# A two-layer decoder for two sequences on one core: norms by column halves, stacks read by halves of the heads, and a new order of steps

## The chip, the core and the metric

The kernel runs on one core of a Trainium2 chip. The metric is the device time of one execution in microseconds, as the median of several runs. The profile shows one execution.

## The reference

The input is x, two sequences of 512 tokens with 128 features (f32), and a small context of 32 tokens per sequence. Two layers of three blocks each are applied, and each block stands inside a residual sum and a plain layernorm:

```python
x = _layernorm(x + L0_attn(x))     # rms norm, gated linear recurrence, rms norm, gated MLP
x = _layernorm(x + L0_xattn(x, ctx, mask))         # attention over the 32 context tokens
x = _layernorm(x + L0_ffn(x))      # x += latent attention(rmsnorm(x)), 16 heads, causal
                                   # x += experts(rmsnorm(x)): 1 shared, 7 routed, best 2
x = _layernorm(x + L1_attn(x))     # selective scan, 16 states
x = _layernorm(x + L1_xattn(x, ctx))  # norm, FiLM by context attention, long convolution
                                   # by FFT, then a norm with an MLP, then a norm
x = _layernorm(x + L1_ffn(x))      # experts: 2 shared, 8 routed, best 2
```

## The kernel before, in words

**Tiles.** A sequence is held feature-major, as tiles of 128 partitions (features) by 512 columns (tokens), f32. The two sequences are lanes a and b; work on weights that both share is lane w. Each lane a and b has four PSUM banks of 128x512, `own(b, 0)` to `own(b, 3)`, and SBUF tiles `A(b, i)`; `Xin[b]` is the running x (x_in in the profile).

**A norm.** A norm sums squares over the partitions. ScalarE (ACT) squares a tile (step `.sq`), TensorE (PE) multiplies it by a matrix of ones so that each partition holds the sum of its column (`.v` or `.ss`, L551-553), ACT takes Ln and then Exp with scale -0.5, which is the inverse root (`.l`, `.r`, L1077-1095), and VectorE (DVE) multiplies (L1418-1420). Two norms, m1 and f1, have an epsilon outside the root and take five steps on ACT (`.sq .l .n .m .r`, L1097-1107). The norms of a lane are h1, h4, ln1 (recurrent block), ln2 (context attention), m1, f1 and ln3 (latent attention and first experts), ln4 (scan), lni, lnf, lno, ln5 (state-space block) and ln6 (second experts). Each step works on the whole 128x512 tile. Ln, Exp, Gelu and Sin need tables that ACT loads by an instruction of its own (L1067).

**Stages of a lane.** Recurrent block (`hawk`); context attention (`xa.*`, a query product, exp, `xa.t`, the output product `xa.o`, the sum `s2`, ln2, `X2`); latents (m1, `lat`, `kf`, `q`); the split of keys and queries into bf16 parts, which SP writes to DRAM (`staged`, L489-496) and reads back as one stack of rows per side (`stacked`, L498-503); 40 max units per lane (`mx0.A` to `mx7.E`: eight pairs of heads, matmuls L688 and L691, DVE reductions L1407, L1549), from which a mask row is made (`nl`, `nmt`) and sent by a DMA; 40 score units `su` (L705, L708) with exp on ACT; first experts (f1, router `rt`, eight units of `fg`, `fu`, `fw`, `fd`, L775, L780, L791, L802, with an ACT step `sl` and DVE steps per unit); ln3; scan (sixteen states, `cn` L843, `bn` L849, `yn` L856 on PE, exp `aa` and copies `bb` on ACT, `by` on POOL (GpSimd), product and recurrence `sc`, L1719, `hc` on DVE); ln4; state-space block (`xb.s` L888, FiLM, Fourier products L870 and L923, centring products `lnf.c` and `ln5.c`, MLP `w1` and `w2`); second experts (14 units of `eg`, `eu`, `ew`, `ed`); ln6 and the store of x (L541-544).

**What sets the order.** Each engine runs one program in order. `STEPS` lists the steps of a lane on each engine; `TURNS` (L187-214) is a string per engine, "a6 w1 a6 ...", that says how the lanes take turns, and `take_turns` (L452-459) issues one step per turn. `TABLES` (L218-221) gives the numbers of the ACT steps ahead of which a table is loaded. Semaphores count the steps of each engine and lane; a step waits for counts. Lane b runs some way behind lane a throughout. SP issues its DMAs in the order of L460-544.

The stacks' reads and the store, as they stand:

```python
stacked("k", b, 0, 4, "hm", 2)
stacked("q", b, 0, 4, "hm", 3)
stacked("k", b, 4, 6, "l", 1)
stacked("q", b, 4, 6, "l", 1)
...
for b in range(B):
    sp.wait_ge(*after("dve", b, "X6"))
    sp.dma_start(out[:, b * T:(b + 1) * T], Xin[b][:, :]).then_inc(stored, 16)
```

## Time and profile before

| | us |
|---|---|
| runs (device time) | 523.45, 525.23, 526.22; median 525.23 |
| the profiled execution | 523.02 |
| its span in the trace | 521.2 |
| PE busy | 442.6 (85% of the span) |
| DVE busy | 362.8 (70%) |
| ACT busy | 288.2 (55%) |
| POOL busy | 127.7 (24%) |
| mean granted TensorE clock | 0.948 of full |

Times in the rows are counted from the span's start. A row of the timeline reads: start, duration, engine, line, operation, output and input tiles with shapes, count, and in brackets the idle time of the engine ahead of it and what released it; consecutive instructions of one kind are one row. A row of the view of groups reads: line, engine, operation, tiles, count, then busy time in us, the mean of one in ns, and the idle time ahead of them with its releasers. A row of the view by stretches of time reads: stretch, its length, busy time (and count of instructions) of PE, PEld (weight loads), DVE, ACT and POOL, then the granted TensorE clock, the share of the DMA engines in use and GB/s. Stretches follow the stages: up to 112.0 the recurrent blocks and context attention of both lanes; to 147.2 a's max units; to 153.0 the mask row of a; 193.5 to 238.7 a's attention done, b's score units with a's first experts; 277.8 the end of a's `dl`, when a's scan begins; 309.6 a's `sc7`; 373.6 b's scan ends; 383.0 b's query product `xb.s`; 423.0 the state-space blocks are done; 514.0 the last expert product.

### The profile page before, as it was taken

The page shows a single profiled execution, that of the slowest core. Times are in us where ns is not written, and L with a number is a line of the kernel's source. Part 1 is how long each engine was busy: PE and PEld are TensorE (multiplying, and loading weights), DVE is VectorE, ACT ScalarE, POOL GpSimd, SP SyncE. Part 2 cuts the span into 40 slices and gives each one's busy share as a digit, 9 for nine tenths or more (in the row PEclk, how much of TensorE's full clock was granted, in tenths as well). Part 3 has the DMA queues.
Part 4 walks back from the last instruction along what each step waited for, and adds up shares of the span by engine and source line. Part 5 has one row for each costly group of instructions (what it writes and reads, how often), then busy time and mean ns, then how long its engine had stood idle before and what let it go on. Part 6 is the DMA issues. An engine that isn't in the chain of part 4 may idle for free.

```text
span 521.2 us, 5808 instructions
## 1 busy us (share of the span) xinstructions
PE 442.6 (85%) x2045; PEld 203.5 (39%) x2045; DVE 362.8 (70%) x625; ACT 288.2 (55%) x443; POOL 127.7 (24%) x128
## 2 busy tenths in 40 slices
PE   6979879478849989999778797778979889999996
PEld 3534423233325534343333332333645434444441
DVE  1496875548937946645988898999694462695774
ACT  5637884431125557887557968686347344722124
POOL 2100000001940009318406868656200000000000
PEclk9999999678769999999999989999989989999998
DMA  8940001830820000004000000160000000000001
GB/s 289 305 148 6 1 1 60 181 133 7 221 24 1 1 6 2 0 2 126 37 1 0 1 1 0 20 241 1 1 0 1 0 0 1 1 0 0 1 1 40
DMA packets 10279, 24.29 MB, mean 47 GB/s; under 512 B 3103, under 2 KB 7936, under 8 KB 9088
## 3 DMA queue, kind: packets, MB, share of 16 engines
q1 hardware_dynamic: 10148, 23.82, 15.4%
q8 instruction: 16, 0.26, 0.2%
q14 instruction: 13, 0.11, 0.1%
q10 hardware_dynamic: 102, 0.10, 0.1%
HBM read 19.88 MB, written 3.67 MB: 45 GB/s over the span
## 4 chain that ended last, share of the span: by engine, by line
PE 54%; DVE 23%; ACT 15%; issue 5%; DMA 2%; DVEq 0%; ACTq 0%
ACT AR L1071 10%; DVE AR L1398 6%; PE PS L802 6%; PE PS L780 6%; PE PS L775 6%; DVE stats L1407 4%; DVE AR L1404 4%; PE PS L705 3%; PE PS L719 3%; ACT L1067 3%; PE PS L589 3%; PE PS L553 3%; DVE AR L1719 3%; PE PS L688 2%; PE PS L870 2%
## 5 line engine op out<-in xcount | busy, mean ns | idle before, releaser
L1071 ACT ACTIVATE AR<-PS 128x512 f32<-128x512 f32 (+1 forms) x201 | 113.1, 593 | 108.9 <-PE PS L775 47.3
L2026 POOL TENSOR_TENSOR AR<-AR 128x512 f32<-128x512 f32 (+2 forms) x48 | 54.2, 1139 | 90.7 <-DVE AR L1398 68.6
L1071 ACT ACTIVATE AR<-AR 128x512 f32<-128x512 f32 (+2 forms) x72 | 43.9, 618 | 51.9 <-DVE AR L1398 34.1
L1398 DVE TENSOR_TENSOR AR<-PS,AR 128x512 f32<-128x512 f32 x74 | 50.4, 687 | 13.8 <-ACT AR L1071 6.4
L1407 DVE TENSOR_REDUCE stats<-PS 128x1 f32<-128x512 f32 (+4 forms) x88 | 43.2, 525 | 13.4 <-PE PS L691 8.1
L1404 DVE SCALAR_TENSOR_TENSOR AR<-AR,PS 128x512 f32<-128x512 f32 x44 | 30.0, 683 | 21.7 <-ACT AR L1071 21.6
L1067 ACT ACT_TABLE_LOAD x33 | 42.3, 1283 | 0.6
L2119 POOL TENSOR_TENSOR RR<-KL,lags 128x512 f32<-128x512 f32 x24 | 31.0, 1324 | 46.5 <-PE PS L708 46.4
L1719 DVE TENSOR_TENSOR_SCAN AR<-PS,AR 128x512 f32<-128x512 f32 x32 | 38.9, 1217 | 2.9 <-ACT PS L1071 2.7
L705 PE MATMUL PS<-RR 100*128 100x512 bf16 (+3 forms) x128 | 31.9, 323 | 7.9 <-DMA RR<-wT 5.5
L688 PE MATMUL PS<-RR 97*128 97x512 bf16 (+3 forms) x128 | 33.4, 335 | 4.0 <-DVE stats L1407 3.1
L856 PE MATMUL PS<-AR,W_sq 128*128 128x512 f32 x64 | 33.8, 610 | 1.8 <-DVE AR L1398 1.8
L1404 DVE SCALAR_TENSOR_TENSOR AR<-PS,AR 128x512 f32<-128x512 f32 x44 | 29.9, 687 | 7.5 <-PE PS L791 4.8
L553 PE MATMUL PS<-AR,W_sq 128*128 128x512 f32 x44 | 25.6, 666 | 10.5 <-ACT AR L1071 10.3
L775 PE MATMUL PS<-x_in,RR 128*128 128x512 f32 x56 | 28.9, 607 | 1.1 <-DVE AR L1404 1.1
L1071 ACT ACTIVATE AR<-PS,W_vec 128x512 f32<-128x512 f32 (+1 forms) x32 | 22.2, 696 | 12.7 <-PE PS L553 7.3
L802 PE MATMUL PS<-AR,RR 128*128 128x512 f32 x56 | 28.5, 593 | 0.2 <-DVE AR L1404 0.2
L780 PE MATMUL PS<-x_in,RR 128*128 128x512 f32 x56 | 27.9, 594 | 0.0
L1398 DVE TENSOR_TENSOR AR<-AR 128x512 f32<-128x512 f32 (+4 forms) x36 | 24.4, 694 | 3.8 <-ACT AR L1071 3.3
L1071 ACT ACTIVATE PS<-AR,W_vec 128x512 f32<-128x512 f32 x32 | 22.0, 690 | 6.5 <-DVE AR L1719 6.4
L691 PE MATMUL PS<-W_bf 128*128 128x256 bf16 (+1 forms) x80 | 22.0, 275 | 0.0
L1549 DVE TENSOR_REDUCE stats<-PS 128x1 f32<-128x384 f32 x32 | 17.6, 550 | 5.2 <-PE PS L691 5.2
(239 smaller groups left out, 768.7 us busy)
## 6 DMA issues: line engine op xcount, KB each, us to landing
RR<-in_ffn SPq DMA_DIRECT2D x1, 2688.0 KB, 9.2
RR<-in_ones SPq DMA_DIRECT2D x2, 832.0 KB
RR<-in_ones SPq DMA_DIRECT2D x2, 784.0 KB
RA<-in_moe SPq DMA_DIRECT2D x1, 1539.5 KB, 6.3
W_mla<-in_mla SPq DMA_DIRECT2D x1, 1504.0 KB, 16.4
W_late<-in_late SPq DMA_DIRECT2D x1, 1076.0 KB, 10.5
RA<-in_xa SPq DMA_DIRECT2D x1, 1056.0 KB, 8.7
RA<-in_hawk SPq DMA_DIRECT2D x1, 1024.0 KB, 10.8
```

The lines of the kernel that those rows point to most:

```text
L688: mm(ring[:, c:c + n_], Qst[b][0:MROWS, h, 128 * qt:128 * qt + 128], Kst[b][0:MROWS, h, 0:n_], start=(qt, c) == segs[0][1:], stop=False)
L705: mm(ring[:, c:c + n_], Kst[b][0:KROWS, h, 128 * kb:128 * kb + 128], Qst[b][0:KROWS, h, 128 * kb:T], start=(c == 0), stop=False)
L775: mm(own(b, 0), w(group, "g", 128 * k, 128), x, start=True, stop=True)\
L780: mm(own(b, 1), w(group, "u", 128 * k, 128), x, start=True, stop=True)\
L802: mm(own(b, 3), w(group, "d", 128 * j, 128), A(b, 6 + j % 2), start=(j == 0 and base is None), stop=(k == n))\
L1067: nc.scalar.preload_act_table_set(tables[loaded[0]])
L1071: nc.scalar.activation(out_, in_, func, bias=bias, scale=scale).then_inc(*done("act", *step))
L1398: nc.vector.tensor_tensor(out_, a, b_, op).then_inc(*done("dve", *step))
L1404: nc.vector.scalar_tensor_tensor(out_, a, s1, b_, op0, op1).then_inc(*done("dve", *step))
L1407: nc.vector.tensor_reduce(out_, a, X, op).then_inc(*done("dve", *step))
L1719: nc.vector.tensor_tensor_scan(A(b, 14 + i % 2), own(b, 3), A(b, 4 + i % 3), 0.0, ALU.mult, ALU.add).then_inc(*done("dve", b, f"sc{i}"))
L2026: nc.gpsimd.tensor_tensor(out_, a, b_, op).then_inc(*done("pool", *step))
```

## The change

- `COLS` names two halves of the columns: "a" for 0 to 255, "" for 256 to 511. Every norm but lni works on them step by step: squares, the product with ones, Ln, Exp, and the DVE multiply are two instructions of 128x256 each. The two halves' sums go into two different PSUM banks of the lane (`NORM_BANKS`). The five-step norms m1 and f1 take ten ACT steps.
- The DVE sums ahead of norms (`s2`, `s4`, `xt`, `s5`, `s6`), the centred products `lnf.x` and `lno.x`, the centring matmuls `lnf.c` and `ln5.c`, and the affine `lnf.g` are halved too. The norms whose input is one product of PE (`shr`, `fd7`, `w2`) wait for the whole of it.
- The last x is stored by four DMAs of 128 KB, one per lane and half, instead of two of 256 KB.
- The stacks are read by halves of the heads: first heads 0 to 7 of all four row groups, then heads 8 to 15, with a semaphore of their own (`second`), for which PE waits ahead of pair 4 of the max units. That is eight DMAs per lane instead of four, with the same bytes.
- `TURNS` and `TABLES` are new. Steps per engine (lanes a and b and w together): PE 611 to 637, DVE 584 to 618, ACT 409 to 491, POOL 96 as before. Table loads by `TABLES`: 33 to 34.

The places where the new order differs most:

- PE: `a.mx0.A` and `a.mx0.B` come before `b.xa.t0` (they were behind `b.xa.o`); `b.mx0.A` to `C` come before `a.su0`; b's mask row is made after `a.su26` (was `a.su32`). By `b.su39` only `a.rt`, `fg0`, `fu0` of a's experts have been issued (before: `fg`, `fu` up to 3, `fw`, `fd` up to 2). The scan of a starts when b has about 8 DVE steps of its experts left (19 before); b's scan starts after `a.sc7` (before: after `a.sc15`). b's `w1`, `w2` come ahead of a's second experts. Lane b is alone from `eg9` (before: from `eg5`), since a's `ln6` and store come before b's last units.
- ACT: the log table is loaded ahead of `a.ln1.l`, another ahead of `b.h4.l`, sin ahead of `b.h4.sq` (early part); all ten steps of b's f1 with two table loads and the shared `sQ0` stand between `a.sl1` and `a.sl2`; log is loaded ahead of `a.ln6.l` and exp again ahead of `b.el10`.
- DVE: the shared centring `v0.s`, `v0.m`, `v0.c` and `k1`, `bi`, `vr` stand in part ahead of `a.gh1` and `a.x1`; b's convolution taps stand behind `a.X1` and `a.xa.m0`.
- POOL: b's split comes before `bf`, `bf1`, `se`, `wz`, `la` and `dc1` of lane w.

```diff
+COLS = (("a", slice(0, HT)), ("", slice(HT, T)))
+NORM_BANKS = {"h1": (0, 1), "h4": (1, 2), "ln1": (1, 2), "ln2": (1, 2), "f1": (0, 3), "ln3": (1, 0), "ln4": (1, 3),
+              "lnf": (3, 0), "lno": (3, 1), "ln5": (3, 2), "ln6": (1, 0), "lnf.c": (2, 1), "ln5.c": (0, 1)}
...
-            def mean_square(b, t, i, step="v"):
-                pe.wait_ge(*after("act", b, f"{t}.sq"))
-                mm(own(b, i), w("sq", "ones"), A(b, 1), start=True, stop=True).then_inc(*done("pe", b, f"{t}.{step}"))
+            def mean_square(b, t, step="v"):
+                for i, (h, c) in zip(NORM_BANKS[t], COLS):
+                    pe.wait_ge(*after("act", b, f"{t}.sq{h}"))
+                    mm(own(b, i)[:, c], w("sq", "ones"), A(b, 1)[:, c], start=True, stop=True)\
+                        .then_inc(*done("pe", b, f"{t}.{step}{h}"))
+                    yield
...
+            def layernorm(b, t, engine, ready, src, bias=0, whole=False):
+                for h, c in COLS:
+                    act.wait_ge(*after(engine, b, ready if whole else ready + h))
+                    f(A(b, 1)[:, c], src(h)[:, c], ACT.Square, (b, f"{t}.sq{h}"), bias=bias)
+                    yield
+                for i, (h, c) in zip(NORM_BANKS[t], COLS):
+                    act.wait_ge(*after("pe", b, f"{t}.v{h}"))
+                    f(A(b, 7)[:, c], own(b, i)[:, c], ACT.Ln, (b, f"{t}.l{h}"), scale=1.0 / D, bias=vec("eps"))
+                    yield
+                for h, c in COLS:
+                    act.wait_ge(*after("act", b, f"{t}.l{h}"))
+                    f(A(b, 7)[:, c], A(b, 7)[:, c], ACT.Exp, (b, f"{t}.r{h}"), scale=-0.5)
+                    yield
...
             def normed(b, t, name, src):
-                dve.wait_ge(*after("act", b, f"{t}.r"))
-                tt(Xin[b][:, :], src, A(b, 7), ALU.mult, (b, name))
+                for h, c in COLS:
+                    dve.wait_ge(*after("act", b, f"{t}.r{h}"))
+                    tt(Xin[b][:, c], src[:, c], A(b, 7)[:, c], ALU.mult, (b, name + h))
+                    yield
...
-                stacked("k", b, 0, 4, "hm", 2)
-                stacked("q", b, 0, 4, "hm", 3)
-                stacked("k", b, 4, 6, "l", 1)
-                stacked("q", b, 4, 6, "l", 1)
+                sp.wait_ge(draft["k", b, "hm"], 16 * 2)
+                stacked("k", b, 0, 4, 0)
+                sp.wait_ge(draft["q", b, "hm"], 16 * 3)
+                stacked("q", b, 0, 4, 0)
+                sp.wait_ge(draft["k", b, "l"], 16)
+                stacked("k", b, 4, 6, 0)
+                sp.wait_ge(draft["q", b, "l"], 16)
+                stacked("q", b, 4, 6, 0)
+                for which in "kq":
+                    stacked(which, b, 0, 4, 1)
+                    stacked(which, b, 4, 6, 1)
...
                 for pair in PAIRS:
+                    if pair == len(PAIRS) // 2:
+                        pe.wait_ge(second["k", b], 16 * 2)
+                        pe.wait_ge(second["q", b], 16 * 2)
...
-                sp.wait_ge(*after("dve", b, "X6"))
-                sp.dma_start(out[:, b * T:(b + 1) * T], Xin[b][:, :]).then_inc(stored, 16)
+                for h, c in COLS:
+                    sp.wait_ge(*after("dve", b, f"X6{h}"))
+                    sp.dma_start(out[:, b * T + c.start:b * T + c.stop], Xin[b][:, c]).then_inc(stored, 16)
...
-        "a6 w1 a6 w2 a1 w1 a8 w1 a1 w2 a2 b1 a3 b2 a1 b2 a2 b4 a2 b1 a2 b8 a1 b1 a3 b1 a1 b10 a2 b1 a10 b1 a3 "
+        "a7 w1 a6 w1 a1 w1 a1 w1 a7 w1 a2 w2 a2 b1 a1 b1 a2 b1 a1 b1 a1 b2 a2 b3 a2 b1 a2 b2 a1 b7 a1 b2 a4 b9 "
...
```

## Rows read from the trace of the kernel before

**Rows 1.** Busy time by stretches of the span, one row per stage.

```profile
94.90:112.00 17.10, 11.38 (x29) 6.04 (x29) 7.26 (x13) 2.90 (x6) 0.00 (x0) 0.50 0.54 92
112.00:147.20 35.20, 27.46 (x124) 10.51 (x122) 31.56 (x69) 8.39 (x13) 16.84 (x28) 0.84 0.54 141
147.20:153.00 5.80, 1.24 (x7) 0.71 (x8) 0.00 (x0) 1.19 (x2) 2.16 (x2) 0.50 0.03 8
...
193.50:238.70 45.20, 43.03 (x299) 19.46 (x300) 25.34 (x45) 38.02 (x63) 23.14 (x18) 0.96 0.00 1
238.70:277.80 39.10, 30.64 (x230) 12.87 (x229) 31.80 (x56) 23.45 (x33) 13.30 (x11) 1.00 0.17 55
277.80:309.60 31.80, 28.86 (x74) 11.67 (x73) 27.62 (x36) 23.69 (x33) 27.27 (x23) 0.95 0.00 1
309.60:373.60 64.00, 51.54 (x313) 24.37 (x312) 59.60 (x71) 43.79 (x72) 38.98 (x29) 1.00 0.15 54
373.60:383.00 9.40, 5.88 (x33) 4.34 (x34) 6.84 (x9) 3.93 (x6) 0.00 (x0) 0.93 0.00 0
383.00:423.00 40.00, 35.58 (x124) 20.50 (x124) 23.05 (x40) 19.95 (x29) 0.00 (x0) 0.93 0.00 0
423.00:514.00 91.00, 89.20 (x228) 38.53 (x227) 60.53 (x112) 34.22 (x51) 0.00 (x0) 1.00 0.00 1
514.00:521.20 7.20, 2.25 (x4) 0.59 (x4) 2.08 (x3) 3.21 (x6) 0.00 (x0) 0.79 0.19 73
```

**Rows 2.** Timeline of the norm h4 of lane a, from squares to multiply.

```profile
37.09 0.63 ACT L1071 ACTIVATE AR<-AR 128x512 f32<-128x512 f32 x1 [6.52 <-DVE AR L1398]
...
38.09 1.12 PE L553 MATMUL PS<-AR,W_sq 128*128 128x512 f32 x2
...
39.25 0.60 ACT L1071 ACTIVATE AR<-PS 128x512 f32<-128x512 f32 x1 [1.53 <-PE PS L553]
...
39.88 0.63 ACT L1071 ACTIVATE AR<-AR 128x512 f32<-128x512 f32 x1
...
40.54 0.75 DVE L1404 SCALAR_TENSOR_TENSOR AR<-AR,W_vec 128x512 f32<-128x512 f32 x1 [1.50 <-ACT AR L1071]
```

**Rows 3.** Groups of instructions, by shape: prices at 512 and at 256 columns.

```profile
L1071 ACT ACTIVATE AR<-PS 128x512 f32<-128x512 f32 x197 | 111.4, 595 | 105.6 <-PE PS L775 47.3 <-PE PS L708 21.5 <-PE PS L849 10.8
...
L1071 ACT ACTIVATE AR<-PS 128x256 f32<-128x256 f32 x2 | 0.6, 371 | 0.0
...
L1398 DVE TENSOR_TENSOR AR<-PS,AR 128x512 f32<-128x512 f32 x74 | 50.4, 687 | 13.8 <-ACT AR L1071 6.4 <-PE PS L606 2.5 <-PE PS L780 2.1
...
L1398 DVE TENSOR_TENSOR stats<-stats 128x256 f32<-128x256 f32 x6 | 2.4, 421 | 0.1
...
L553 PE MATMUL PS<-AR,W_sq 128*128 128x512 f32 x44 | 25.6, 666 | 10.5 <-ACT AR L1071 10.3
...
L923 PE MATMUL PS<-RR,AR 128*128 128x256 f32 x32 | 8.9, 431 | 0.0
...
L1067 ACT ACT_TABLE_LOAD x33 | 42.3, 1283 | 0.6
```

**Rows 4.** Timeline: last stack read of lane a, `b.xa.t0`, first max unit of a.

```profile
95.46 0.42 SPq L503 DMA_DIRECT2D RR<-draft_q  x1
...
104.05 1.11 PE L636 MATMUL PS<-W_sq,AR 128*128 128x128 f32 x4 [3.11 <-DVE AR L1398]
...
110.18 0.15 PEld L688 LDWEIGHTS PS<-RR 97*128 97x128 bf16 x1 [0.52 <-issue]
```

**Rows 5.** Timeline: PE's first score unit of lane a, behind the mask row.

```profile
152.39 0.61 PE L705 MATMUL PS<-RR 100*128 100x512 bf16 x1 [4.56 <-DMA RR<-wT]
```

**Rows 6.** Timeline: a table load between steps of b's f1; POOL's shared work in the scan.

```profile
252.27 1.28 ACT L1067 ACT_TABLE_LOAD   x1
...
285.31 4.06 POOL L2119 TENSOR_TENSOR RR<-KL,lags 128x512 f32<-128x512 f32 x4
```

**Rows 7.** Timeline: PE's product `xb.s` of lane b, behind its norm ln4.

```profile
380.89 0.49 PE L888 MATMUL PS<-M,x_in 128*128 128x128 f32 x2 [3.52 <-DVE x_in L1398]
```

More of the change, by code:

```diff
@@ L141 @@
[L141 removed]
+        *_halves("ln4.v"), "xb.s", "xb.t", "fl0", "fl1", "fl2", "fl3", "xit",
+        "xf0", "xf1", "inv0", "inv", *_halves("lnf.c"), *_halves("lnf.v"), "w10", "w11", "w12", "w13", "w2", *_halves("lno.v"), *_halves("ln5.c"), *_halves("ln5.v"),
         "rt1", *[x for k in range(UB1 + 1) for x in unit_steps(k, UB1, SH1, "e")],
[L143 removed]
+        *_halves("ln6.v")],
     "act": [
[L145 removed]
@@ L299, in build @@
                   "sel1", "km", "kr", "tm"]}
+        second = {(w, b): ctx.enter_context(nc.semaphore(f"second_{w}{b}")) for w in "kq" for b in range(B)}
         stack = {(w, b): ctx.enter_context(nc.semaphore(f"stack_{w}{b}")) for w in "kqm" for b in range(B)}
@@ L858, in scan @@
                         yield
[L859 to L860 removed]
+                yield from mean_square(b, "ln4")
             def forward(o, p, x):
@@ L926, in state_space @@
                     yield
-                pe.wait_ge(*after("dve", b, "xt"))
-                mm(own(b, 2), w("sq", "Cm"), A(b, 0), start=True, stop=True).then_inc(*done("pe", b, "lnf.c"))
-                yield
-                mean_square(b, "lnf", 3)
-                yield
+                for i, (h, c) in zip(NORM_BANKS["lnf.c"], COLS):
+                    pe.wait_ge(*after("dve", b, f"xt{h}"))
+                    mm(own(b, i)[:, c], w("sq", "Cm"), A(b, 0)[:, c], start=True, stop=True)\
+                        .then_inc(*done("pe", b, f"lnf.c{h}"))
+                    yield
+                yield from mean_square(b, "lnf")
                 pe.wait_ge(*after("act", b, "lnf.g"))
@@ L946, in state_space @@
                 yield
-                mean_square(b, "lno", 3)
-                yield
-                pe.wait_ge(*after("dve", b, "lno.x"))
-                mm(own(b, 1), CmG, A(b, 9), start=True, stop=True).then_inc(*done("pe", b, "ln5.c"))
-                yield
-                mean_square(b, "ln5", 0)
-                yield
+                yield from mean_square(b, "lno")
+                for i, (h, c) in zip(NORM_BANKS["ln5.c"], COLS):
+                    pe.wait_ge(*after("dve", b, f"lno.x{h}"))
+                    mm(own(b, i)[:, c], CmG, A(b, 9)[:, c], start=True, stop=True).then_inc(*done("pe", b, f"ln5.c{h}"))
+                    yield
+                yield from mean_square(b, "ln5")
             def second_experts(b):
@@ new lines, in root_mean_square @@
+            def root_mean_square(b, t):
+                for i, (h, c) in zip(NORM_BANKS[t], COLS):
+                    act.wait_ge(*after("pe", b, f"{t}.ss{h}"))
+                    f(A(b, 7)[:, c], own(b, i)[:, c], ACT.Ln, (b, f"{t}.l{h}"), scale=1.0 / D)
+                    yield
+                for h, c in COLS:
+                    act.wait_ge(*after("act", b, f"{t}.l{h}"))
+                    f(A(b, 7)[:, c], A(b, 7)[:, c], ACT.Exp, (b, f"{t}.r{h}"), scale=-0.5)
+                    yield
@@ L1152, in hawk @@
                     yield
-                yield from layernorm(b, "ln1", "pe", "shr", own(b, 0), 1)
+                yield from layernorm(b, "ln1", "pe", "shr", lambda h: own(b, 0), whole=True)
             def context_attention(b):
@@ L1247, in first_experts @@
                 yield from gates(b, U0, SH0, "f", "sl", "h", "wt", E0)
-                yield from layernorm(b, "ln3", "pe", f"fd{U0}", own(b, 3), 1)
+                yield from layernorm(b, "ln3", "pe", f"fd{U0}", lambda h: own(b, 3), whole=True)
             def scan(b):
@@ L1318, in state_space @@
                 yield
-                yield from layernorm(b, "lnf", "pe", "lnf.c", own(b, 2), 3)
-                affine(b, "lnf", 9, 2, "gff", "bff")
-                yield
+                yield from layernorm(b, "lnf", "pe", "lnf.c", lambda h: own(b, NORM_BANKS["lnf.c"][0 if h else 1]))
+                for h, c in COLS:
+                    affine(b, "lnf", 9, 2, "gff", "bff", h, c)
+                    yield
                 for k in range(4):
@@ L1325, in state_space @@
                     yield
-                yield from layernorm(b, "lno", "pe", "w2", own(b, 2), 3, b2c)
-                yield from layernorm(b, "ln5", "dve", "s5", A(b, 0), 0)
+                yield from layernorm(b, "lno", "pe", "w2", lambda h: own(b, 2), b2c, whole=True)
+                yield from layernorm(b, "ln5", "dve", "s5", lambda h: A(b, 0))
             def second_experts(b):
```

260 lines of the change are left out of this document (126 added, 134 removed), and 52 rows, old and new, of tables (STEPS, TABLES, TURNS).

## The prediction

> **What bounds the kernel.** I first split the span into stages and read, in the view by stretches, which engine fills each one [rows 1]. No engine bounds the whole. In a's attention with b's score units PE is full (43.03 of 45.2 us), and in the second experts again (89.20 of 91). DVE is full in a's max units (31.56 of 35.2) and in the scans (27.62 of 31.8, 59.60 of 64.0), and it is the busiest engine of the first experts' stretch (31.80 of 39.1). Nobody is full in three places: 94.9 to 112.0, where PE works 11.38 of 17.1 us at half clock (1.2 GHz); 147.2 to 153.0, the wait for a's mask row; and around the norms of b at 373.6 to 383.0 and of both lanes up to 423.0. There the chain of one norm sets the time. So I read a norm in the timeline [rows 2]: squares at 37.09, the multiply done at 41.29, 4.2 us for five instructions on three engines, each waiting for the one before it. A shorter chain pays only where no engine is full. That is the whole question.
>
> **What a half costs.** ACT takes 595 ns for 512 columns and 371 for 256, DVE 687 and 421, a matmul pass of PE 666 and 431 [rows 3]. Two halves thus cost 147 ns more than the whole on ACT and 155 on DVE. A chain in halves: squares 2 x 0.37, then PE's second half, 0.43 and the hand-over (the wait of 1.53 us for a product of two passes, of which 1.12 are busy, so 0.41 + 2 x 0.3, as the passes overlap: about 1.0), then Ln, Exp, multiply of the second half, 0.37 + 0.39 + 0.45. That is 2.95, with a little queueing 3.1: **1.1 us gained per exposed chain** of the 4.2. Between 0 (an engine in the chain is busy with other steps, or the input comes whole) and 1.9 (the next product starts on its first half, which no reader of the whole tile does). I take 1.1, nearest to the row.
>
> The Trainium skill, "VectorE: DVE Perf Modes", section on the TRN2 errata, speaks against the change: operations that read SBUF on VectorE and ScalarE pay a fixed cost per instruction, and tiles of 512 elements or more are advised. The durations of 371 and 421 ns agree with a fixed part. By that advice alone the change would be a loss of the extra busy time, which the next paragraph prices from rows.
>
> The extra busy time is 82 x 0.147 = 12.1 us on ACT and 34 x 0.155 = 5.3 on DVE. ACT is full nowhere [rows 1], so its part costs only inside chains, where the 3.1 has it. Of DVE's, some 12 of the 34 pairs lie in stretches where DVE is full: about 1.9 us, in the terms below.
>
> **Part by part, along the span.**
>
> 1. *Start to 112.0.* Four chains of a and four of b are crossed, in part hidden by the other lane; I count 4 x 1.1 = 4.4 gained. Against it: two table loads move into chains (2 x 1.28 [rows 3] = 2.6), the shared centring stands on DVE ahead of `a.x1` (about one step of 0.7), and b's taps behind `a.X1` hold `a.xa.m0`'s successors for about 1.0. Net 0, between -3 (the loads fall into waits) and +2. `a.mx0.A` and `B` now stand ahead of `b.xa.t0` on PE. Before, `b.xa.t0` ran at 104.05, and the last read of a's stacks was issued at 95.46 [rows 4], while the first max unit came at 110.18. If the stacks come later than b's exps, everything of b behind them waits; half-stacks are half the bytes, so I take this as nothing, up to +2 inside this term.
> 2. *112.0 to 147.2.* DVE-bound. b's latents no longer stand in its way as whole tiles, and two waits of DVE on chains (3.6 idle of 35.2) shrink: -1.5, between -2.5 and 0.
> 3. *147.2 to 153.0.* a's mask row. PE idles 4.56 us for it [rows 5]. `b.mx0.A` to `C` now stand in that hole, because half of b's stacks suffices. a's 40 max units fill 35.2 us with 27.46 of PE [rows 1], so three are 2.1 us of PE, taken out of a later stretch where PE is full; half of it, as the mask row also has to be made with b's units in its way: -1.0, between -4.6 and 0.
> 4. *Experts and scans, 193.5 to 373.6.* Two units of a's experts and the first two products of a third move from ahead of `b.su39` to behind it. In the second experts 28 units fill 89.2 us of PE, 3.2 each [rows 1], so that is at most 2 x 3.2 + 2 = 8.4; 7.5 taken, since those 89.2 hold a router and norms too. The attention becomes shorter by them and the stretch behind longer. In that one PE has 39.1 - 30.64 = 8.5 idle, so in principle they fit; but b's f1 takes ten half steps (10 x 0.38), two loads (2 x 1.28 [rows 6]) and `sQ0` (1.9) on ACT between `a.sl1` and `a.sl2`: 8.3 us in which a's experts get no sigmoid part. The five steps of f1 in halves gain nothing in length, as each engine step waits for ACT anyway. In the scan, POOL's shared pieces stand as a block of 4.06 [rows 6] between a's `by`. DVE, which is the bound, has the same work, and the two experts side by side give it more to choose from, which gives back some. Net +1.5, between -3 and +7.5 (nothing of the moved work fits).
> 5. *ln4 of b, to 383.0.* PE waited 3.52 for it [rows 7], and in the stretch DVE and PE are both part idle. Sum, squares, product, root and multiply in halves: 1.1, and 0.5 more as `s4` is halved too, and b comes out of the scan with less left of a's work in the way. -2, between -3.5 and 0.
> 6. *383.0 to 423.0.* PE is idle 4.4 of 40.0 [rows 1], on lnf, lno and ln5. Three chains of each lane with centring and affine in halves, of which two are exposed: -2, between -4.4 and 0.
> 7. *End.* a's ln6 products move into the PE-bound stretch (the whole one is 1.12 busy [rows 2]: +0.9), two table loads (2.6) stand between `b.el9` and `b.el10` where a unit lasts 3.2, which covers most (+0.7), and the tail of 7.2 us [rows 1] holds one lane's norm in halves and stores of 128 KB (-1.3). +0.3, between -1.3 and +1.6.
>
> The reads by halves alone (term 1 and 3) I cost at nothing: the last was issued 14.7 us ahead of the first use [rows 4], and the bytes are the same.
>
> **Sum.** 0 - 1.5 - 1.0 + 1.5 - 2 - 2 + 0.3 = -4.7. The profiled execution took 523.0, so 518.3 in its terms. It lies 2.2 below the median of the runs, 525.2. I forecast **520.5 us**, 0.9% below the median. What this measurement can tell from no change is 0.5%, that is 522.6 to 527.9.
>
> **Rivals.**
> - *The clock comes back (chance 0.17).* From 94.9 to 112.0 the clock is half, with PE busy 11.38 us [rows 1]. If the max units drawn forward keep PE at work, and the full 2.4 GHz stays, up to 5.7 us of this falls away, and the hole at 147.2 may go as well. For it: max units are the one work that is ready. Against it: the chains of b still stop PE, and two units are short. Term 1 at -4 and term 3 at -3.2 give 6.2 less: 514.3.
> - *Halves give back what they gain (0.20).* The exposed chains are hidden by the other lane already, DVE pays its 5.3, and terms 2, 3, 5 and 6 (6.5) come out at half while term 4 costs 3: 525.2 - 3.2 + 3 + 0.3 = 525.3, no difference. It holds too if the change does not do what it says: reads by halves of stacks that had long been issued.
> - *a's experts are late (0.23).* Slower. One mechanism: term 4 at its bound. The 8.3 us of ACT between `a.sl1` and `a.sl2` lie on a's path, `a.dl` comes up to 7.5 later, and the scans, where DVE is full for 87.2 of 95.8 us, can't take it back. It decides from the point at which `a.dl` comes later than 281. Then term 4 is +7.5, the others at half of their gain (-3.1): 525.2 + 4.4 = 529.6.
>
> **How the numbers follow.** Forecast 0.40, clock 0.17, no difference 0.20, late experts 0.23. Faster by over 0.5% is the forecast and the clock, 0.57; within it 0.20; slower 0.23. The range: the clock's case and term 5 and 6 at their better ends (2.4 and 1.5 less) reach 510.4, and the late experts with term 1 at +2 reach 531.6. So 510 to 532, with less than 2 in 10 outside. The forecast's own range is 516 to 524.
>
> **What would show it.** In the changed kernel: ACT groups of 128x256 near 0.37 to 0.40 us and a norm of about 3.1 us from first square to last multiply (term by chain); `b.s2` within 2 us of 112; PE's idle time ahead of the first score unit below 4; `a.dl` at 276 to 281; DVE still over 90% busy in the scans; the wait ahead of `xb.s` below 2.5; the tail from the last product at about 6. The forecast falls if `a.dl` is past 281 and the scans don't make up for it, if the stretch around 95 to 112 shows full clock, or if PE waits for DMA ahead of `b.xa.t0`.

## The result: 1.2% slower, and the profile after

The changed kernel's median is 530.95 us (527.53 to 536.00, 9 runs), the kernel before's 524.96 (520.94 to 526.53, 9 runs beside it). The ratio is 1.0121, with a 95% interval of 1.0089 to 1.0152. The forecast was 520.5, 0.9% faster. The time lies inside the range of 510 to 532, on the wrong side of no change, and within 1.5 us of the rival "a's experts are late" (529.6, chance 0.23).

Two of the changed kernel's nine runs, 535.49 and 536.00, are over 1.5% above its fastest, count as slow and are left out of the ratio; the other seven lie within 5.5 us (527.53 to 533.02), as far apart as the 5.6 of the kernel before. The profiled execution took 530.81 us, with a span of 529.0. The two profiles differ by 7.8 us and the medians by 6.0, since the profile before was a quick one; the times by steps below are those of the profiles.

The view by stretches for the changed kernel follows, with stretches that end at the same steps as those of [rows 1] where the same step ends one: `b.s2` at 118.8, a's mask row from DVE at 152.8, `a.su0` at 158.6, `a.su39` at 203.5, `b.su39` at 230.5, `a.dl` at 288.4, the end of a's scan (348.1) and of b's (384.5), `b.xb.s` at 392.3, then up to 432, to the last product (523.0) and to the end. The columns are those of [rows 1].

```profile
101.70:118.80 17.10, 10.73 (x30) 5.12 (x29) 7.49 (x15) 4.57 (x10) 0.00 (x0) 0.61 0.58 106
118.80:152.80 34.00, 26.53 (x124) 11.40 (x125) 31.75 (x70) 8.53 (x21) 16.62 (x30) 0.85 0.56 146
152.80:158.60 5.80, 2.98 (x14) 1.57 (x15) 1.64 (x4) 1.19 (x2) 4.98 (x8) 0.50 0.03 8
158.60:203.50 44.90, 42.27 (x376) 22.54 (x377) 26.04 (x63) 28.88 (x53) 0.00 (x0) 0.98 0.01 2
203.50:230.50 27.00, 25.42 (x217) 11.84 (x210) 10.93 (x20) 21.84 (x47) 12.15 (x12) 1.00 0.01 2
230.50:288.40 57.90, 51.21 (x288) 22.46 (x288) 52.06 (x93) 34.39 (x53) 20.53 (x18) 1.00 0.12 37
288.40:348.10 59.70, 43.90 (x199) 16.95 (x200) 53.70 (x60) 40.74 (x63) 50.34 (x39) 0.86 0.00 1
348.10:384.50 36.40, 32.35 (x202) 18.95 (x188) 32.49 (x43) 22.93 (x41) 14.58 (x10) 1.00 0.27 94
384.50:392.30 7.80, 5.10 (x20) 3.57 (x20) 6.17 (x10) 4.25 (x9) 0.00 (x0) 0.77 0.00 0
392.30:432.00 39.70, 35.26 (x139) 22.91 (x139) 21.49 (x39) 23.58 (x45) 0.00 (x0) 0.96 0.00 1
432.00:523.00 91.00, 89.22 (x236) 39.81 (x234) 62.56 (x127) 38.11 (x63) 0.00 (x0) 1.00 0.01 3
523.00:529.00 6.00, 1.13 (x4) 0.67 (x4) 1.50 (x4) 2.26 (x6) 0.00 (x0) 0.98 0.13 44
```

The kernel before has these rows for the two attentions and the scans, cut at the same steps (its stretch from `b.su39` to `a.dl` stands in [rows 1]):

```profile
153.10:195.80 42.70, 40.06 (x331) 21.38 (x330) 28.33 (x66) 24.77 (x44) 0.00 (x0) 0.94 0.01 2
195.80:238.70 42.90, 40.76 (x289) 18.05 (x288) 25.34 (x45) 36.83 (x61) 23.14 (x18) 0.98 0.00 1
...
277.80:333.40 55.60, 45.59 (x243) 18.16 (x241) 49.44 (x61) 41.41 (x60) 45.09 (x37) 0.97 0.01 2
333.40:373.60 40.20, 34.81 (x143) 17.88 (x143) 37.79 (x46) 26.07 (x45) 21.17 (x15) 1.00 0.23 82
```

Every step counts a semaphore, so the trace tells when each step ended. The difference of these times says where the 7.8 us of span went:

| step | before | after | difference | gained or lost since the step above |
|---|---|---|---|---|
| `a.g3` (gate products of a) | 23.73 | 28.34 | +4.61 | +4.6 |
| `b.s2` | 112.04 | 118.80 | +6.76 | +2.2 |
| `a.nl` (mask row of a, DVE) | 147.16 | 152.72 | +5.56 | -1.2 |
| `a.su0` | 153.11 | 158.64 | +5.53 | 0.0 |
| `a.dl` | 277.80 | 288.37 | +10.57 | +5.0 |
| `b.hc15` (b's scan on DVE) | 373.56 | 384.45 | +10.89 | +0.3 |
| `b.xb.s` | 383.06 | 392.28 | +9.22 | -1.7 |
| `b.X6` | 518.76 | 526.72 | +7.96 | -1.3 |

Two stretches lose: the start (+6.8), and the way from `a.su0` to the end of the scans (+5.4). The rest gains 4.2. These are differences from one profile before to one after. How far a difference can be trusted is seen in the other traces of the study, wherever their order is the same in the stretch; where they change the reading, it is said below.

The halves themselves cost what the forecast's rows said. From the groups by shape:

```profile
L1093 ACT ACTIVATE AR<-PS 128x256 f32<-128x256 f32 x26 | 9.3, 378 | 4.8 <-PE PS L952 2.4 <-PE PS L828 1.1 <-PE PS L639 0.7
...
L578 PE MATMUL PS<-AR,W_sq 128*128 128x256 f32 x88 | 27.9, 429 | 13.0 <-ACT AR L1093 8.6 <-DMA W_sq<-in_sq 4.4
...
L1431 DVE TENSOR_TENSOR x_in<-AR 128x256 f32<-128x256 f32 x16 | 6.3, 420 | 5.2 <-ACT AR L1093 5.2
```

And the norm h4 of lane a, in the timeline, is the chain of [rows 2]:

```profile
42.20 0.72 ACT L1093 ACTIVATE AR<-AR 128x256 f32<-128x256 f32 x2 [7.02 <-DVE AR L1431]
...
42.67 1.13 PE L578 MATMUL PS<-AR,W_sq 128*128 128x256 f32 x4 [0.60 <-ACT AR L1093]
...
43.41 0.82 ACT L1093 ACTIVATE AR<-PS 128x256 f32<-128x256 f32 x2 [0.48 <-PE PS L578]
...
44.12 0.71 ACT L1093 ACTIVATE AR<-AR 128x256 f32<-128x256 f32 x2
44.56 0.88 DVE L1437 SCALAR_TENSOR_TENSOR AR<-AR,W_vec 128x256 f32<-128x256 f32 x2 [1.21 <-ACT AR L1093]
```

It takes from 42.20 to 45.44, 3.24 us instead of 4.20. PE's idle time ahead of the product with ones is 0.60, and ACT's ahead of Ln is 0.48 instead of 1.53.

### The profile page after: what moved, and what is told of

It reads as the page before. It is cut to its first block, busy times and chain, and to the rows that moved or that the text cites. A ratio compares the mean times of both kernels' runs of the same rounds, so it can differ in the third digit from the quotient of the medians.

```text
span 529.0 us, 6043 instructions
## 1 busy us (share of the span) xinstructions
PE 448.7 (85%) x2097; PEld 216.3 (41%) x2097; DVE 367.2 (69%) x659; ACT 296.2 (56%) x526; POOL 122.1 (23%) x128
## 4 chain that ended last, share of the span: by engine, by line
PE 53%; DVE 23%; ACT 13%; issue 6%; DMA 2%; SPq 1%; ACTq 0%; DVEq 0%
ACT AR L1093 9%; DVE AR L1431 6%; PE PS L801 5%; PE PS L828 5%; PE PS L806 4%; DVE stats L1440 4%; DVE AR L1437 4%; PE PS L880 3%; PE PS L615 3%; PE PS L728 3%; ACT L1089 3%; PE PS L742 3%; PE PS L893 2%; PE PS L578 2%; DMA x_in<-in_x 2%
## 5 line engine op out<-in xcount | busy, mean ns | idle before, releaser
L1093 ACT ACTIVATE AR<-PS 128x512 f32<-128x512 f32 (+1 forms) x213 | 114.5, 575 | 127.5 <-PE PS L801 60.4
L1093 ACT ACTIVATE AR<-AR 128x256 f32<-128x256 f32 (+3 forms) x114 | 48.4, 462 | 46.5 <-DVE AR L1431 30.6
L1431 DVE TENSOR_TENSOR AR<-PS,AR 128x512 f32<-128x512 f32 (+1 forms) x76 | 50.1, 670 | 14.0 <-ACT AR L1093 5.4
L2160 POOL TENSOR_TENSOR RR<-KL,lags 128x512 f32<-128x512 f32 x24 | 25.5, 1100 | 67.2 <-PE PS L731 45.3
L578 PE MATMUL PS<-AR,W_sq 128*128 128x256 f32 x88 | 27.9, 429 | 13.0 <-ACT AR L1093 8.6
L880 PE MATMUL PS<-AR,W_sq 128*128 128x512 f32 x64 | 35.1, 639 | 0.0
L728 PE MATMUL PS<-RR 100*128 100x512 bf16 (+3 forms) x128 | 29.6, 305 | 3.1 <-ACT AR L1093 2.3
L1431 DVE TENSOR_TENSOR AR<-AR 128x512 f32<-128x512 f32 (+4 forms) x36 | 25.5, 723 | 6.6 <-ACT AR L1093 6.0
L1093 ACT ACTIVATE AR<-PS,W_vec 128x256 f32<-128x256 f32 (+2 forms) x48 | 25.0, 549 | 8.4 <-PE PS L578 4.1
L578 PEld LDWEIGHTS PS<-AR,W_sq 128*128 128x128 f32 x88 | 16.0, 203 | 28.4 <-ACT AR L1093 21.0
```

What stands on the lines that cost most here:

```text
L578: mm(own(b, i)[:, c], w("sq", "ones"), A(b, 1)[:, c], start=True, stop=True)\
L728: mm(ring[:, c:c + n_], Kst[b][0:KROWS, h, 128 * kb:128 * kb + 128], Qst[b][0:KROWS, h, 128 * kb:T], start=(c == 0), stop=False)
L880: mm(own(b, 2), w("sq", "Cm"), A(b, 12 + (i - 1) % 2), start=(i == 1), stop=(i == NS))\
L1093: nc.scalar.activation(out_, in_, func, bias=bias, scale=scale).then_inc(*done("act", *step))
L1431: nc.vector.tensor_tensor(out_, a, b_, op).then_inc(*done("dve", *step))
```

## Where the start lost 4.6 us

In the timeline of the changed kernel, DVE, ACT and PE stand like this between 13 and 28 us. The second block is PE's row in the kernel before:

```profile
13.65 0.43 DVE L1446 CAST AR<-kmask 128x512 f32<-128x512 uint8 x1 [5.23 <-DMA tmask<-in_tm]
14.04 0.42 ACT L1093 ACTIVATE AR<-x_in 128x256 f32<-128x256 f32 x1 [6.30 <-DMA x_in<-in_x]
19.52 8.80 PE L615 MATMUL PS<-AR,RA 128*128 128x512 f32 x16 [3.72 <-DVE AR L1437]
```

```profile
16.61 7.11 PE L589 MATMUL PS<-AR,RA 128*128 128x512 f32 x16 [0.86 <-DVE AR L1404]
```

Two steps of other lanes stand ahead of a's convolution in the new order, and each waits for a DMA: on DVE the cast of a mask, `w.km`, ahead of a's taps, and on ACT the first half of b's square, `b.h1.sqa`, ahead of the two copies `a.cv0`, `a.cv1` that the taps read. The engines run in order, so lane a waits with them. Its gate products start 2.9 us late, and the same 16 matmul passes then take 8.80 us instead of 7.11. The granted clock says why. The two blocks are the view by stretches from 19 to 24 us, after and then before; the granted clock is 0.66 of full in the one and 1.00 in the other:

```profile
19.00:24.00 5.00, 4.48 (x7) 1.97 (x8) 0.83 (x2) 2.83 (x7) 0.00 (x0) 0.66 0.93 224
```

```profile
19.00:24.00 5.00, 5.00 (x14) 2.09 (x14) 0.69 (x1) 3.94 (x8) 1.42 (x4) 1.00 0.94 207
```

## Experiments

Each kernel is built from one of the two by a change of the order or of the code. "Halves" is the code of the changed kernel. Where an order of one kernel is used with the code of the other, a whole step stands where its second half stood, or two halves side by side where the whole stood. Each ratio is to the kernel before as it ran beside that experiment, with a median from 521.03 to 524.98 us; it is estimated from the single runs, so it isn't the exact quotient of two medians.

**Halves alone.** The changed code in the old order.

```diff
 # code of the changed kernel
-TURNS, TABLES of the changed kernel
+TURNS, TABLES of the kernel before, each halved step's turn doubled
```

> All halves, the two banks, the stacks read by halves and the four stores, in the order of before (each pair of half steps stands where the whole step stood, table loads as before). Theory 'order' (the new order of steps costs the time): the halves gain what exposed chains gave in the forecast, about 1.1 us per exposed norm, so about 520, 1% below before. Rival 'halves' (their fixed costs, 12 us of ACT and 5 of DVE, make the loss): about 530, as the changed kernel.

Measured: 521.50 us, ratio 0.9988 (0.9965 to 1.0011). The halves are not the loss. Over the whole kernel they are no gain that can be told either, though 1% was expected.

**Order alone.** The code of before in the new order.

```diff
 # code of the kernel before
-TURNS, TABLES of the kernel before
+TURNS, TABLES of the changed kernel, the turn of each first half taken out
```

> The new order and table loads with whole norms, whole stacks and two stores (each whole step stands where its second half stood). Theory 'order': slower than the changed kernel, since nothing is gained on the chains: 533 or more. Rival 'halves': as before, 525.

Measured: 536.62 us, ratio 1.0294 (1.0257 to 1.0331). The loss is the order's. In the new order the halves are worth 1.0294 - 1.0121 = 1.7%, in the old one 0.1%. One thing differs from the changed kernel besides the halves: b's first square stands here behind a's copies, where its second half stood, and a's gate products end at 24.80, not at 28.34. So this 2.9% holds little of the wait at the start.

That can be read in the length of the chains, from the end of the step that feeds a norm to the end of its multiply, in us:

| chain | before | order alone | both (changed) | halves alone |
|---|---|---|---|---|
| a: `x1` to `xn2` (h4) | 4.23 | 3.92 | 3.27 | 3.80 |
| a: `shr` to `X1` (ln1) | 4.77 | 6.27 | 6.24 | 4.84 |
| b: `xa.o` to `X2` (ln2) | 4.90 | 6.08 | 6.88 | 4.49 |
| a: `x2a` to `xf` (f1) | 7.72 | 11.77 | 12.11 | 7.65 |
| b: `yn16` to `X4` (ln4) | 6.10 | 4.75 | 3.77 | 6.17 |
| b: `xt` to `lnf.g` (lnf) | 10.76 | 7.63 | 4.66 | 8.32 |
| b: `ed14` to `X6` (ln6) | 4.75 | 4.74 | 3.77 | 4.47 |

Side by side in the old order a chain gains 0.4 us at h4 and ln2, 0.3 at ln6, 2.4 at lnf, and nothing at ln1 and ln4, where other work of ACT or DVE stands in it. At ln4 and ln6 only the new order gives the halves their 1 us (4.75 to 3.77, 4.74 to 3.77). The same new order makes other chains longer: ln1 of a, because a table load of 1.28 us (at 55.62) and a shared Tanh (`th`, 0.30) stand in it, and f1 of a, by 4.4 us, because the score units of b come first.

The lengths of whole stretches add what the chains don't show. From the end of b's scan to `b.X6`, the kernel before takes 145.2 us, halves alone 143.0, order alone 148.0 and the changed kernel 142.3. Behind the scans the halves are thus worth 2.2 us in the old order too, and the new order adds 0.7 with them and costs 2.8 without. The clock has a part in it: in all five traces of kernels without halves PE stands at half clock for 3.4 or 6.8 us from a point between 418 and 430 us, where the state-space blocks hand over to the second experts, and in none of the eleven with halves. Halves alone give their 2.2 us back ahead of that: `a.su0` is 1.0 later than before, and the way from there to the end of the scans 1.2 longer (221.6 against 220.4), both within what traces of one order differ by.

**The mask cast put back, in the changed kernel.** TURNS of DVE.

```diff
-a2 w1 a6 w1 a2 w8 ...
+a8 w2 a2 w8 ...
```

> The changed kernel with one shared DVE step, the cast of a mask (km), put back behind lane a's six convolution taps. The trace of the changed kernel shows DVE waiting 5.23 us for the mask's DMA in front of it, and the gate products of a ending 4.6 us later. Theory 'order', first part: the 4.6 us are carried to the end nearly whole, so 4 us less, about 527. Rival 'covered later': the delay is taken up by the waits behind it (DMA of the stacks, mask row), so under 1 us less, 530 to 531.

Measured: 530.92 us, ratio 1.0161 (1.0124 to 1.0198). No gain. In its trace the taps start where ACT's copies let them, and the gate products are still 4.3 us late. PE waits 3.19 us ahead of them.

**The mask cast moved forward, in the kernel before.** TURNS of DVE.

```diff
-a7 w2 a2 w8 ...
+a1 w1 a6 w1 a2 w8 ...
```

> The kernel before with that one step moved ahead of lane a's convolution taps, nothing else. Theory 'order', first part: 4 us more, about 529. Rival 'covered later': within 1 us of before.

Measured: 526.59 us, ratio 1.0095 (1.0064 to 1.0126). The medians show the expected loss. In its trace only 1.1 us of it stand at `a.g3` and at `a.su0` (24.82 and 154.24); where the rest arises isn't shown.

**Both put back, in the changed kernel.** TURNS of DVE as above, and of ACT.

```diff
-a1 w1 a3 w1 a2 b1 w1 a2 ...
+a1 w1 a3 w1 a2 w1 a2 b1 ...
```

> The changed kernel with two early steps put back: the mask cast behind a's taps on DVE, as in the run before, and b's first half square (h1.sqa) behind a's two convolution copies on ACT, where the kernel before had it. In the trace of the changed kernel ACT waits 6.3 us for b's x in front of those copies, and everything of lane a stands behind it. Theory 'early wait': a's gate products end 4 us sooner, and 3 to 4 us of it reach the end, so about 527.5 against 531. Rival 'covered later': a's start is early but a.su0 comes no sooner than 157, and the end moves by less than 1.5 us.

Measured: 528.14 us, ratio 1.0057 (1.0023 to 1.0091), about 3.4 us better than the changed kernel (1.0121; the intervals just meet). PE now waits 0.86 ahead of the gate products:

```profile
16.24 3.67 PE L614 MATMUL PS<-AR,RA 128*128 128x512 f32 x8 [0.86 <-DVE AR L1436]
```

But these are the first 8 passes only, and `a.g3` still ends at 25.00, 1.3 us later than in the kernel before. A third step of another lane is in the way:

```profile
17.68 0.31 ACT L1092 ACTIVATE AR<-AR 128x128 f32<-128x128 f32 x1 [3.14 <-DMA AR<-in_s4d]
18.00 1.28 ACT L1088 ACT_TABLE_LOAD   x1
...
21.29 3.70 PE L614 MATMUL PS<-AR,RA 128*128 128x512 f32 x8 [1.38 <-ACT AR L1092]
```

It is `w.dt`, an Exp on state-space weights that a DMA still brings. In the new order it stands, with a table load, ahead of a's two Gelu steps `gg0` and `gg1`, and the third gate product waits for `gg1`. In the kernel before, `w.dt` comes behind them and ends at 21.00, and `gg1` at 16.39, not 21.25. No run puts this step back alone.

**The square alone put back, in the changed kernel.** The ACT line of the edit above.

> The changed kernel with b's first half square (h1.sqa) behind a's two convolution copies on ACT; the mask cast stays early. Theory 'ACT waits for b's x': all of the gain of the run with both moved, ratio to before about 1.006 against 1.012 to 1.016, so 3 us less than the changed kernel. Rival 'both needed': DVE waits for the mask in its place, and under 1 us is won.

Measured: 531.60 us, ratio 1.0116 (1.0077 to 1.0155). No gain that can be told, though its interval meets that of the run with both put back. The traces say it more sharply: the first gate product (`a.g0`) ends at 22.68 in the changed kernel, at 21.66 with the cast put back, at 21.67 with the square put back, and at 18.21 with both (18.58 before). So the rival holds, "both needed": either wait by itself holds the taps, and taking one away uncovers the other.

**The square moved forward, in the kernel before.** TURNS of ACT.

```diff
-a1 w1 a3 b1 a3 w3 ...
+a1 w1 a1 b1 a5 w3 ...
```

> The kernel before with b's square h1.sq ahead of a's two convolution copies on ACT, nothing else. Theory 'ACT waits for b's x': the copies wait for the DMA until 14 us instead of starting near 12, PE idles in front of the gate products and drops to the lower clock; 3 to 5 us slower, ratio 1.006 to 1.010. Rival 'covered later': under 1 us.

Measured: 529.83 us, ratio 1.0093 (1.0056 to 1.0130). One ACT step two places earlier costs as much in the medians as the mask cast did. The gate products of these two runs, of the square's and then of the cast's:

```profile
20.51 6.18 PE L587 MATMUL PS<-AR,RA 128*128 128x512 f32 x7 [4.80 <-DVE AR L1402]
```

```profile
17.70 7.10 PE L587 MATMUL PS<-AR,RA 128*128 128x512 f32 x16 [2.36 <-DVE AR L1402]
```

With 2.36 us of idle time PE kept its clock (7.10 us for the 16 passes, as before); with 3.33 (square alone put back, 8.74 us for 16), 3.72 and 4.80 it came back at a lower one.

**Old order up to a's first score unit, then the new one.** Halves.

```diff
+order[e] = old[e][steps done at 153.5 us] + new[e][the rest]
```

> Halves throughout; up to the first score unit of a (153 us) each engine's order of before, and from there the order of the changed kernel (steps already done left out). Theory 'both parts lose': the early 5.5 us are gone, the later part loses as in the changed kernel, so 525 to 527. Rival 'early part alone': 521.5, as halves in the old order. Rival 'late part alone': 530.

Measured: 525.76 us, ratio 1.0025 (1.0006 to 1.0044).

**New order up to there, then the old one.** Halves.

```diff
+order[e] = new[e][steps done at 158.0 us] + old[e][the rest]
```

> The mirror of it: halves; up to a's first score unit the order of the changed kernel, from there the order of before. Theory 'both parts lose': 526 to 528 (5.5 us from the early part, less what b's max units, which are ahead, give back). Rival 'early part alone': 530. Rival 'late part alone': 521.5.

Measured: 527.75 us, ratio 1.0081 (1.0045 to 1.0116). Against halves alone (0.9988) the early part costs 0.9% and the late one 0.4%, and together they make 1.3%, as in the changed kernel. The late 0.4% is small for its noise, as the intervals of this pair just meet (1.0006 and 1.0011). The length from `a.su0` to the end of the scans is clearer: 221.6, 221.7 and 223.3 us in three traces with halves and the old order there, 225.8 to 227.9 in six with the new one. So both parts lose.

**Old order up to the end of b's attention, then the new one.** Halves.

```diff
+order[e] = old[e][steps done at 239.6 us] + new[e][the rest]
```

> Halves; the order of before up to b's last score unit (239.6 us), the order of the changed kernel from there. Theory 'DVE work moved out of the attention' (in the changed order the DVE does 37 us of work during both attentions against 54 before, and the 17 us come back in a stretch where DVE is full): with the old order up to here nothing is moved, so no later than halves alone, 521 to 522, or a little less as the new order's tail is shorter. Rival 'order of experts and scans' (the two experts side by side, b's f1 chain on ACT, POOL's pieces): 525 or more, as when the new order starts at 153.

Measured: 537.97 us, ratio 1.0284 (1.0248 to 1.0320). The expected 521 to 522 are missed; the rival's "525 or more" is met, but by 13 us more. The trace shows that this hybrid makes a mismatch of its own. In the old attention a's experts have come to `sl3` when b's last score unit ends (236.40 and 237.51). The new order is written for a b whose score units end 18.6 us ahead of `a.sl3`. It puts b's f1 norm, its two table loads and `b.sl0` ahead of `a.sl4` on ACT:

```profile
246.60 0.72 ACT L1090 ACTIVATE AR<-AR 128x256 f32<-128x256 f32 x2 [2.73 <-DVE AR L1428]
247.34 1.28 ACT L1086 ACT_TABLE_LOAD   x1
...
252.27 1.28 ACT L1086 ACT_TABLE_LOAD   x1
...
260.16 0.60 ACT L1090 ACTIVATE AR<-PS 128x512 f32<-128x512 f32 x1 [2.54 <-PE PS L798]
```

`a.sl4` ends at 260.8, 16.5 us later than in the kernel before, and `a.dl` at 294.6. It says that the order of the experts only fits the attention that it was written with; it does not say what that order costs in its own place.

**New attention alone.** Halves; old up to `a.su0`, new up to `b.su39`, then old.

```diff
+order[e] = old[e][to 153.5 us] + new[e][to 226.7 us] + old[e][the rest]
```

> Halves; old order up to a's first score unit, the changed kernel's order up to b's last score unit (226.7 us), then the old order. Theory 'DVE work moved out of the attention': 524 to 526, all of the late loss. Rival 'order of experts and scans': 521.5.

Measured: 525.71 us, ratio 1.0053 (1.0025 to 1.0082). By the medians the new order of the attentions alone costs as much as the whole late part did (1.0025, the intervals meet). By the traces it is about half: from `a.su0` to the end of the scans 224.0 us, against 221.6 in halves alone and 226.8 with the whole late part new. So the order of the experts and scans has a share too, and no run measures that in its own place. The stretches of this run, from `a.su39` on, cut at `b.su39`, at `a.dl` and at the end of the two scans:

```profile
198.10:225.20 27.10, 25.52 (x218) 11.91 (x218) 10.89 (x21) 22.22 (x48) 12.15 (x12) 1.00 0.01 2
225.20:280.30 55.10, 43.36 (x260) 18.56 (x259) 43.02 (x83) 34.56 (x51) 19.56 (x16) 0.94 0.13 39
280.30:335.80 55.50, 45.58 (x246) 18.63 (x244) 49.62 (x62) 41.64 (x63) 45.13 (x37) 0.97 0.01 3
335.80:377.00 41.20, 34.86 (x144) 18.33 (x144) 38.83 (x48) 26.24 (x48) 20.89 (x15) 1.00 0.22 80
```

b's attention is over 13.5 us sooner than before, counted from `a.su0`, with the same small share of DVE as in the changed kernel (10.89 of 27.1). Behind it DVE has 131.5 us of work in 151.8, against 119.0 in 134.9. That is 87% of the stretch and not more than the 88% before: the stretch grows by 16.9 us with 12.5 us more of DVE work, so DVE's work explains most of its growth but not all.

**b.v ahead of the mask row, in the changed kernel.** TURNS of ACT.

```diff
-... b5 a5 b31 a1 b1 a29 b1 a3 ...
+... b5 a5 b32 a30 b1 a3 ...
```

> The changed kernel with one ACT step moved: the copy of b's values (b.v), whose product is there at 134.8, ahead of a's mask row copy (a.nmt) instead of behind it and its DMA issue. In the trace of the changed kernel b's first max unit waits for it until 156.2, so that only three units fit into the hole. Theory 'b.v holds the units back': they start 2.7 us sooner and their DVE steps too, DVE idle of 4.25 falls to under 2; worth 0.5 to 1 us at the end if DVE's part counts, 0 if not, since PE's next step waits for the mask row anyway. Rival: slower by the copy of 0.6 us ahead of the mask row, no, since ACT waits 13 us there; so none.

Measured: 532.12 us, ratio 1.0140 (1.0094 to 1.0185), no different from the changed kernel. b's first max unit does end earlier (4.6 us ahead of the end of `a.su0` instead of 1.7), and no gain follows from it.

**Halves in the old order, with five max units in the hole.** TURNS of PE and ACT.

```diff
-pe:  ... a3 b4 a28 b1 a2 b1 a1 b1 a2 b1 a1 b2 a2 b2 ...
+pe:  ... a3 b4 a26 b5 a8 b1 a2 b2 ...
-act: ... b2 a1 b27 a1 b1 a37 b1 a4 ...
+act: ... b2 a1 b28 a38 b1 a4 ...
```

> Halves in the order of before, with b.v ahead of a.nmt on ACT and five of b's max units (mx0.A to E) ahead of a's first score unit on PE, where before stood none; nothing else. The first halves of b's stacks landed at 144.5 in the run of halves alone, so five units of about 0.6 us fit into the 4.6 us in which PE waits for the mask row. Theory: 5 x 0.55 = 2.7 us of PE leave the attention, where PE is full, so 518.5 to 519.5, 0.5% under before. Rival 'DVE or the mask row sets it': no difference to halves alone, 521.5.

Measured: 521.59 us, ratio 0.9967 (0.9948 to 0.9986). It is the one kernel of the study whose interval lies below the kernel before. But that interval meets that of halves alone, and from `a.su0` to the end its trace takes the same time as theirs within 0.1 us. The stretches of this run, and then those of halves alone, from a's mask row to `a.su0` and 6.9 us on, show where a part of the expected 2.7 us may go:

```profile
144.90:150.80 5.90, 4.45 (x20) 2.35 (x21) 3.25 (x7) 0.59 (x1) 2.27 (x2) 0.50 0.03 8
150.80:157.70 6.90, 6.59 (x29) 2.07 (x28) 0.23 (x1) 4.05 (x7) 0.00 (x0) 0.52 0.01 2
```

```profile
148.30:154.10 5.80, 1.32 (x7) 0.76 (x8) 0.00 (x0) 1.19 (x2) 2.16 (x2) 0.50 0.03 8
154.10:161.00 6.90, 6.90 (x46) 3.74 (x44) 3.55 (x8) 4.19 (x8) 0.00 (x0) 0.76 0.01 2
```

The units run at half clock. With them the clock stays near half for the 6.9 us behind `a.su0` (0.52); without them it comes back in the middle (0.76), with 46 matmuls instead of 29 in the same 6.9 us. That the units cause this isn't shown. In this trace the full clock returns 6.6 us behind `a.su0`; in eight traces with the old order and no units it returns 1.5 to 4.9 behind it, but in six with the new order up to there, and three or more units, 1.5 to 6.6.

**Stacks by halves alone, in the kernel before.**

```diff
-                stacked("k", b, 0, 4, "hm", 2)
-                stacked("q", b, 0, 4, "hm", 3)
-                stacked("k", b, 4, 6, "l", 1)
-                stacked("q", b, 4, 6, "l", 1)
+                sp.wait_ge(draft["k", b, "hm"], 16 * 2)
+                stacked("k", b, 0, 4, 0)
...
+                for which in "kq":
+                    stacked(which, b, 0, 4, 1)
+                    stacked(which, b, 4, 6, 1)
```

> The kernel before with the stacks read by halves of the heads, nothing else. Theory: the first halves land some 5 us sooner, the last no later than 1 us after the whole did, and nobody waits for either: ratio 0.998 to 1.002. Rival 'twice the DMAs cost SP and the queues': the later half lands after the fifth pair of max units would start, and 1 us or more is lost.

Measured: 524.68 us, ratio 0.9991 (0.9968 to 1.0013). a's first halves have landed at 101.7 and 103.0, the second at 105.6 and 107.7; whole, they had landed at 104.9 and 106.4. Nobody waits for either.

## Why the prediction was wrong

*Start to `b.s2`: forecast 0, at most +2; measured +6.8.* This step failed. It priced what stands in the chains and not what stands ahead of them. The order was compared where a norm is; the two steps of other lanes that moved in front of a's taps were not looked at, though both read a tile that a DMA still fills. In the kernel before, they stand behind a's taps and copies: the cast waits for nothing, and the square waits 1.60 us for x, which holds up no tap. Put back together they give 3.4 us in the medians, and `a.g3` comes 3.3 sooner in the trace. The other 1.3 of the 4.6 at `a.g3` agree with the 1.38 that PE waits behind the third such step, `w.dt`. The clock made the wait dearer: 2.9 us of wait became 4.6. The remaining 2.2 us to `b.s2` are the ones that the forecast did list: one table load and `th` in ln1 of a (1.5 us longer) and DVE's shared steps ahead of b's. How the 2.2 divide between them isn't shown. They are not won back by the chains, of which h4 of a gives 1.0 and b's h4 none (4.26 before, 4.61 after). "Four chains at 1.1" counted norms that are not alone on their engines.

*To `a.nl`: forecast -1.5, measured -1.2.* The number agrees by luck. From `b.s2` to `a.nl` the kernel before takes 35.1 us and the changed one 33.9, but five other traces with the new order there take 33.9 to 35.9, and eight others with the old one 34.5 to 36.4. A gain of this size isn't shown.

*The hole: forecast -1.0, measured 0.0.* The place was right, the worth wrong. In the changed kernel b's units start at 156.21, not at 153.4, because the copy of b's values stands on ACT behind the mask row's copy and the 1.34 us of its DMA issue:

```profile
154.10 1.34 ACTq L1229 DMA_DIRECT2D RR<-wT  x1
...
155.55 0.60 ACT L1093 ACTIVATE Vaug<-PS 128x512 f32<-128x512 f32 x1 [1.48 <-POOL KL L2067]
156.21 0.61 PE L711 MATMUL PS<-RR 97*128 97x512 bf16 x1 [2.82 <-ACT Vaug L1093]
```

Mending that gave nothing. Five units in the hole gave nothing behind it either: from `a.su0` to the end it is 364.6 us with and without them. They run at half clock; whether they also put off its return stays open.

*Experts and scans: forecast +1.5, at most +7.5; measured +5.4 (`a.su0` to `b.hc15`).* This is the other step that failed, by size and by its engine. It asked whether PE has room for the moved experts ("8.5 idle, so in principle they fit"), in a stretch whose own row says that DVE is the busy one. The DVE rows give the account. In both attentions DVE did 28.33 + 25.34 = 53.7 us of work before, and 26.04 + 10.93 = 37.0 after: 16.7 us of DVE work left a place where PE was the bound. The attentions are 13.7 us shorter (71.9 against 85.6). From `b.su39` to the end of the scans DVE does 138.3 us instead of 119.0, and is busy 90% of 154.0 us instead of 88% of 134.9. That stretch is 19.1 longer: 5.4 us net. That DVE's work sets the length is read from these rows; no run changes it alone. The run with the new attention alone lost as much as the whole late part in the medians, and 2.4 of 5.2 us in the traces. The rival "a's experts are late" named the right symptom: `a.dl` at 288.4, past its mark of 281, and its 529.6 is near. Its mechanism was not shown. `a.sl1` to `a.sl2` did grow from 7.9 to 10.5 us, but `a.fg2`, which `a.sl2` reads, was itself ready only 0.5 us before b's norm left ACT (244.16 and 244.64; the same 0.5 with the old start). With the table load behind the norm, ACT's share is some 1.8 us. Most of the rest is on DVE, where other steps stand between those of a's router: its last step `a.wl` ends 4.0 us after `a.sl1`, not 1.9. This too is read from the timeline and not tested.

*ln4: forecast -2, measured -1.7.* Right. b's ln4 chain is 6.10, then 3.77, and the order frees it: with halves in the old order it is 6.17.

*The rest: forecast -2 + 0.3, measured -1.3.* Right in the number, and by the halves alone. From `b.xb.s` to the end the kernel before takes 135.7 us, halves in the old order 132.7 and the changed kernel 134.4. The new order costs 1.7 here that the halves hide. The tail from the last product is 7.2, then 6.0.

*The stacks by halves at nothing: right* (0.9991).

*The clock coming back* (chance 0.17) went the other way: 0.948 mean before, 0.938 after. *Halves that give back what they gain* is what the halves alone do in the old order (0.9988): 2.2 us gained behind the scans, 2.2 lost ahead of their end. Which cause the loss has, covered chains or the extra busy time (6 us on ACT and 4 on DVE), no run tells. The Trainium skill, "VectorE: DVE Perf Modes", section on the TRN2 errata, advises against tiles under 512 elements. The trace agrees with its fixed part (420 ns for 256 columns, 687 for 512), and the runs show that it did not decide here: in the new order the halves were worth 1.7%.

What stays open: how the 1% that `w.km` or `b.h1.sq` costs alone divides between the wait and the clock in the median, as one profile of a kernel can differ from the next by 3 us. Halves alone and the run with the old start have the same order up to 153 us, and `a.x1` ended at 39.0 in the one and 36.0 in the other; 1.5 of that stood already at `a.g3` (24.2 and 22.7), and the other 1.5 came with a clock dip at 34.5. So single steps under 3 us are taken from medians or from lengths within one chain here.

## What to carry to other kernels

In an order written by hand for in-order engines, look at each step that moved ahead of another lane's work for the DMA that it waits for, before any price is put on the steps themselves; such waits side by side hide each other, so take all of them away before the effect is judged. When work moves between stretches, do the sum on the engine that is full where it arrives, not on the one that it leaves. Halving a chain pays where the chain is alone on its engines; there it paid about 1 us of 4.2 to 4.7, and 0 to 0.4 in most others. And compare a new order with the new code in the old order, not with the old kernel alone, or the code's gain hides what the order costs.
